# Head attention of a perceiver block: the values written straight into the projection's layout instead of through copies and moves

## The reference

```
qkv = x @ Wqkv.T + bqkv                      # x: layernorm of the rows, 8 x 64 x 512
qkv = qkv.reshape(B, 16, S, 96)              # a plain reshape: no transpose of heads
q, k, v = split(qkv, 3)                      # 32 numbers each
attn = softmax(q @ k.T / sqrt(32))
vals = (attn @ v).reshape(B, S, 512)
x = x + vals @ Wo.T + bo
```

## Time and profile before

| | us |
|---|---|
| three timed executions | 916.1, 907.73, 914.78 (median 914.78) |
| the profiled execution | 909.06 |
| its span, first to last instruction | 907.3 |
| head attention in it | 702.9 to 779.0 |
| granted TensorE clock, mean of the span | 0.932 |
| busy: PE, DVE, ACT, POOL | 770.9, 598.9, 365.4, 162.7 |

### The profile page before, as it was taken

The page is one execution under the profiler, slowest core; times in us unless marked ns, Lnnn a source line. Parts: engine busy times, 40 slices in busy tenths (PEclk is TensorE's granted clock), DMA queues, the critical chain, the costliest instruction groups (busy, mean ns, idle before and its releaser), DMA issues. The chain is left out here.

```text
span 907.3 us, 37926 instructions
## 1 busy us (share of the span) xinstructions
PE 770.9 (85%) x17278; PEld 642.7 (71%) x17278; DVE 598.9 (66%) x1152; ACT 365.4 (40%) x732; POOL 162.7 (18%) x431
## 2 busy tenths in 40 slices
PE   5697779998989999979998989796788887749995
PEld 2544779998989998979998889796644764324442
DVE  3877457776775876784876785637565878783325
ACT  3776425333525334434334431101157763352331
POOL 3020210411321311311211311101001013140003
PEclk9799889999999999999999999999889788779998
DMA  9976990365291553490463490602294701643425
GB/s 334 375 156 120 263 161 5 56 91 171 42 206 70 77 102 139 64 242 12 67 114 137 65 180 4 143 4 94 85 359 105 233 13 25 207 138 91 122 80 152
DMA packets 180187, 115.76 MB, mean 128 GB/s; under 512 B 146556, under 2 KB 158900, under 8 KB 176828
## 3 DMA queue, kind: packets, MB, share of 16 engines
q1 hardware_dynamic: 169040, 100.85, 46.0%
q10 hardware_dynamic: 8988, 6.69, 2.4%
q0 software_dynamic: 2000, 5.80, 2.2%
HBM read 61.94 MB, written 12.85 MB: 82 GB/s over the span
## 5 line engine op out<-in xcount | busy, mean ns | idle before, releaser
L1036 PE MATMUL banks<-qa,ctxT 128*128 128x64 f16 x3744 | 117.4, 194 | 13.9 <-DVE qa L740 6.5
L1036 PEld LDWEIGHTS banks<-qa,ctxT 128*128 128x128 f16 x3744 | 114.3, 99 | 15.7 <-DVE qa L740 7.5
L987 PEld LDWEIGHTS banks<-wall,whhT 128*128 128x128 f16 x3456 | 110.0, 99 | 10.4 <-issue 3.5
L987 PE MATMUL banks<-wall,whhT 128*128 128x64 f16 x3456 | 112.0, 195 | 3.7 <-issue 2.2
L987 PE MATMUL banks<-qa,wall 128*128 128x64 f16 x3456 | 105.1, 193 | 4.2 <-DVE qa L787 2.8
L987 PEld LDWEIGHTS banks<-qa,wall 128*128 128x128 f16 x3456 | 102.5, 98 | 4.6 <-DVE qa L787 3.0
L1055 PE MATMUL banks<-qa,wall 128*128 128x64 f16 (+1 forms) x1872 | 95.2, 200 | 9.3 <-issue 6.6
L1055 PEld LDWEIGHTS banks<-qa,wall 128*128 128x128 f16 (+1 forms) x1872 | 94.0, 103 | 10.6 <-issue 10.6
L1055 PE MATMUL banks<-wall 128*128 128x64 f16 (+1 forms) x936 | 94.0, 199 | 2.3 <-issue 2.3
L1055 PEld LDWEIGHTS banks<-wall 128*128 128x128 f16 (+1 forms) x936 | 88.1, 103 | 2.4 <-issue 2.4
L88 POOL TENSOR_TENSOR wall<-wall 128x64 f32<-128x64 f32 x24 | 12.3, 513 | 349.7 <-DVE wall L83 349.7
(11 more groups left out here) (279 smaller groups left out, 1492.8 us busy)
## 6 DMA issues: line engine op xcount, KB each, us to landing
wall<-in_ctx_dram SPq DMA_DIRECT2D x17, 1024.0 KB, 10.5
wall<-in_L_ffn_routed_w_dram SPq DMA_DIRECT2D x23, 512.0 KB, 8.3
unit<-in_ctx_dram SPq DMA_DIRECT2D x6, 1024.0 KB, 7.4
xg_scratch<-room SPq DMA_DIRECT2D x1, 3840.0 KB, 20.5
y_scratch<-room ACTq DMA_DIRECT2D x15, 256.0 KB, 2.0
ctxT<-in_L_xattn_gru_wih_dram SPq DMA_DIRECT2D x3, 1024.0 KB, 17.7
ctxT<-in_L_xattn_gru_whh_dram SPq DMA_DIRECT2D x1, 3072.0 KB, 26.1
ctxT<-in_L_attn_Wqkv_dram SPq DMA_DIRECT2D x12, 256.0 KB, 8.1
```

The lines of the kernel that those rows point to most:

```text
L987: mm = pe.matmul(dst[o], a, b, start=start, stop=True, skip_group_check=True)
L1036: mm = pe.matmul(score[n][:, t * K:(t + 1) * K], a, q, start=(k == 0), stop=(k == 3 * DC - 1), skip_group_check=True)
```

## The change

`values(k)` makes for each group four products in place of one: product ii takes those columns of the turned scores that belong to quarter ii of the projection's chunk (`pT_chunks`, 32 columns in runs of 4) and writes them to partitions 32 ii to 32 ii + 31, a column tile of its own. The values of a batch then lie in PSUM as 128 partitions x 256, in one bank for each parity of k. From there `vals_high(k)` on ScalarE and `vals_low(k)` on VectorE make the two f16 halves, once for each batch in place of once for each tile. `values_out`, the 16 transfers of `move_values` and their semaphores go. `project(t)` moves in TensorE's order from batch 2t + 4 to batch 2t + 3 (ahead of that batch's values), the third of them from behind the loop into batch 7; `add_y(t)` moves on VectorE from batch 2t + 5 to batch 2t + 4. In the tail the halves of the last values stand ahead of `add_y(RT - 2)` and of the remaining chunks of weights, in place of behind two of the split tiles. The halves are written in runs of 4 f16 numbers.

```diff
--- before.py
+++ after.py
@@ -1464,14 +1464,12 @@
         prob, halves, pT = (words(big.ctxT[0])[:, i * third:(i + 1) * third] for i in range(3))
         prob, pT = (a.rearrange("p (s g q) -> p s g q", s=2, g=GB) for a in (prob, pT))
         valsS = halves.bitcast(F16).rearrange("p (s c t) -> p s c t", s=2, c=DC)
-        vals = vT
-
-        valsT = slots.rearrange("p t c r -> p (t c r)").rearrange("p (c t) -> p c t", c=DC)
-
...
         var_out, seeded, root_out, pool_done = (sem(n) for n in ("var_out", "seeded", "root_out", "pool_done"))
         var, rstd, tmp, more = (e_all.root[:, j] for j in range(4))
@@ -1479,13 +1477,15 @@
         def turn_bank(t):
             return e_all.psum[:, t % 2]
 
-        moved = [sem(f"moved{t}") for t in range(RT)]
+        def values_of(k):
+
+            return value[:, k % 2, 0:4 * 64].rearrange("p (m c r) -> p m c r", c=DC, r=4)
+
+        def values_half(k, i):
+
+            return valsS[:, i, :, 64 * k:64 * k + 64].rearrange("p c (m r) -> p m c r", r=4)
 
         block = ctx.enter_context(nc.Block())
-
-        def move_values(eng, t, ii):
-            eng.dma_start(valsT[32 * ii:32 * ii + 32, :, t * P:(t + 1) * P],
-                          vals[:, ii:HC:4, t * P:(t + 1) * P]).then_inc(moved[t], 16)
 
         @block.sync
         def _(sp):
@@ -1495,11 +1495,6 @@
...
-            for t in range(RT):
-
-                sp.wait_ge(vals_out, 4 * (t + 1))
-                for ii in range(4 if t + 1 < RT else 2):
-                    move_values(sp, t, ii)
 
         @block.gpsimd
         def _(pool):
@@ -1524,19 +1519,19 @@
             def v_in(k):
                 act.wait_ge(v_turned, k + 1)
                 if k >= 2:
-                    act.wait_ge(valued, 2 * (k - 1))
+                    act.wait_ge(valued, k - 1)
                 act.copy(v[:, k % 2].rearrange("p g e -> p (g e)"), vb[:, 0:GB * HD]).then_inc(v_out, 1)
 
             def probs_turned(k):
                 for j in range(2):
                     act.wait_ge(prob_turned, 2 * k + j + 1)
                     if k >= 2:
-                        act.wait_ge(valued, 2 * (k - 1))
+                        act.wait_ge(valued, k - 1)
                     act.copy(pT[:, k % 2, 4 * j:4 * j + 4, :].rearrange("p g q -> p (g q)"), probT[:, j, :]).then_inc(pT_out, 1)
 
-            def vals_high(t):
-                act.wait_ge(moved[t], 64)
-                act.copy(valsS[:, 0, :, t * P:(t + 1) * P], valsT[:, :, t * P:(t + 1) * P]).then_inc(vals_hi, 1)
+            def vals_high(k):
+                act.wait_ge(valued, k + 1)
+                act.copy(values_half(k, 0), values_of(k)).then_inc(vals_hi, 1)
 
             def exponentials(k):
                 act.wait_ge(shifted, k + 1)
@@ -1552,22 +1547,19 @@
                 if k + 2 < B:
                     q_block(act, h, qT, k + 2)
                 v_in(k)
+                if k >= 1:
+                    vals_high(k - 1)
                 probs_turned(k)
                 if k + 1 < B:
                     exponentials(k + 1)
                 if k + 2 < B:
                     v_block(k + 2)
-                if k >= 3 and k % 2 == 1:
-                    vals_high((k - 3) // 2)
                 if 2 <= k < B - 1:
                     wall_high(act, e_all, IN_PROJECT + k - 2, IN_PROJECT + k - 1)
-            act.wait_ge(vals_out, 4 * RT)
-            for ii in range(2, 4):
-                move_values(act, RT - 1, ii)
+            vals_high(B - 1)
             wall_high(act, e_all, IN_PROJECT + B - 3, IN_PROJECT + B - 1)
             for t in range(2):
                 tile_high(act, e_all, turn_bank(t), t)
-            vals_high(RT - 1)
             wall_high(act, e_all, IN_PROJECT + B - 1, IN_HEADS)
             tile_high(act, e_all, turn_bank(2), 2)
 
@@ -1594,17 +1586,9 @@
                                             total[half].unsqueeze(2).to_broadcast([64, GB, 64]), ALU.mult)
                     ins.then_inc(prob_out, 1)
 
-            def values_out(k):
-                for j in range(2):
-                    dve.wait_ge(valued, 2 * k + j + 1)
-                    t0 = 64 * k + 32 * j
-                    dst = vals[:, :, t0:t0 + 32].rearrange("e c (m r) -> e m c r", r=4)
-                    dve.tensor_copy(dst, value[0:HD, j, :].rearrange("e (m c r) -> e m c r", c=HC, r=4)).then_inc(vals_out, 1)
-
-            def vals_low(t):
-                dve.wait_ge(vals_hi, t + 1)
-                dve.tensor_tensor(valsS[:, 1, :, t * P:(t + 1) * P], valsT[:, :, t * P:(t + 1) * P],
-                                  valsS[:, 0, :, t * P:(t + 1) * P], ALU.subtract).then_inc(vals_lo, 1)
+            def vals_low(k):
+                dve.wait_ge(vals_hi, k + 1)
+                dve.tensor_tensor(values_half(k, 1), values_of(k), values_half(k, 0), ALU.subtract).then_inc(vals_lo, 1)
 
             def add_y(t):
                 dve.wait_ge(y_done, t + 1)
@@ -1631,20 +1615,17 @@
                     dve.wait_ge(e_all.rw_hi, 1)
                     dve.scalar_tensor_tensor(e_all.rw16[:, :, 1], e_all.rw[:], WS, e_all.rw16[:, :, 0], ALU.mult, ALU.subtract)\
                         .then_inc(e_all.rw_lo, 1)
-                if k >= 5 and k % 2 == 1:
-                    add_y((k - 5) // 2)
+                if k >= 4 and k % 2 == 0:
+                    add_y((k - 4) // 2)
                 if k >= 1:
-                    values_out(k - 1)
-                if k >= 3 and k % 2 == 1:
-                    vals_low((k - 3) // 2)
+                    vals_low(k - 1)
                 if k >= 3:
                     wall_low(dve, e_all, IN_PROJECT + k - 3, IN_PROJECT + k - 2)
-            values_out(B - 1)
+            vals_low(B - 1)
             add_y(RT - 2)
             wall_low(dve, e_all, IN_PROJECT + B - 3, IN_PROJECT + B - 1)
             for t in range(2):
                 tile_low(dve, e_all, turn_bank(t), t)
-            vals_low(RT - 1)
             wall_low(dve, e_all, IN_PROJECT + B - 1, IN_HEADS)
             add_y(RT - 1)
             tile_low(dve, e_all, turn_bank(2), 2)
@@ -1670,17 +1651,18 @@
 
             def values(k):
                 pe.wait_ge(v_out, k + 1)
-                for j in range(2):
-                    pe.wait_ge(pT_out, 2 * k + j + 1)
-                    if k >= 1:
-                        pe.wait_ge(vals_out, 2 * (k - 1) + j + 1)
-                    for g in range(4):
-                        mm = pe.matmul(value[0:HD, j, g * P:(g + 1) * P], v[:, k % 2, 4 * j + g, :],
-                                       pT[:, k % 2, 4 * j + g, :], start=True, stop=True)
-                    mm.then_inc(valued, 1)
+                if k >= 2:
+                    pe.wait_ge(vals_lo, k - 1)
+                for g in range(GB):
+                    if g % 4 == 0:
+                        pe.wait_ge(pT_out, 2 * k + g // 4 + 1)
+                    for ii in range(4):
+                        mm = pe.matmul(value[32 * ii:32 * ii + 32, k % 2, 32 * g:32 * g + 32], v[:, k % 2, g, :],
+                                       pT_chunks[:, k % 2, g, ii], start=True, stop=True)
+                mm.then_inc(valued, 1)
 
             def project(t):
-                pe.wait_ge(vals_lo, t + 1)
+                pe.wait_ge(vals_lo, 2 * (t + 1))
                 if t >= 1:
                     pe.wait_ge(y_out, t)
                 n = 0
@@ -1695,10 +1677,9 @@
                 turn_probs(k)
                 if k + 2 < B:
                     head_scores(pe, h, kT, k + 2)
-                if k >= 4 and k % 2 == 0:
-                    project((k - 4) // 2)
+                if k >= 3 and k % 2 == 1:
+                    project((k - 3) // 2)
                 values(k)
-            project(RT - 2)
             pe.wait_ge(shifted, B)
             for t in range(2):
                 turn_tile(pe, c, e_all, turn_bank(t), t)
```

More of the change, by code:

```diff
@@ L1466, in head_attention @@
         valsS = halves.bitcast(F16).rearrange("p (s c t) -> p s c t", s=2, c=DC)
-        vals = vT
-        valsT = slots.rearrange("p t c r -> p (t c r)").rearrange("p (c t) -> p c t", c=DC)
-        bo_in, zeroed, v_ready, v_turned, v_out, expd, prob_out, prob_turned, pT_out, valued, vals_out, \
+        pT_chunks = pT.rearrange("p s g (h c ii r) -> p s g ii h c r", h=2, ii=4, r=4)
+        bo_in, zeroed, v_ready, v_turned, v_out, expd, prob_out, prob_turned, pT_out, valued, \
             vals_hi, vals_lo, y_done, y_out, bo_added, dve_done = (sem(n) for n in (
                 "bo_in", "zeroed", "v_ready", "v_turned", "v_out", "expd", "prob_out", "prob_turned",
-                "pT_out", "valued", "vals_out", "vals_hi", "vals_lo", "y_done",
+                "pT_out", "valued", "vals_hi", "vals_lo", "y_done",
                 "y_out", "bo_added", "dve_done"))
```

## The result

The changed kernel takes 905.69 us (median of 16 runs, 899.53 to 912.15), the kernel before, in the same comparison, 912.77 us (16 runs, 907.73 to 919.49). The ratio is 0.9928 with a 95% interval of 0.9907 to 0.9950: faster, by 0.5 to 0.9%, so the whole interval lies within the 1% that the prediction called "same". The forecast was 903, and 905.69 lies in its range, but "faster" by more than 1%, which it held the likeliest (0.51), didn't come. The profiled executions took 909.06 before and 905.73 after, with spans of 907.3 and 904.0. The saving was 7 us in place of 9.1, and the rest of this document is mostly about why it wasn't 9.1 and what came to light on the way.

A forecast was written before the change was run, and what follows sets the result against it. No engine was full; the softmax's circle, 4.85 us by itself, was lengthened by VectorE's copies, waits for high halves and TensorE's gaps. Saving 9.1 us, 6.6 at the last product and 2.5 in the tail, counted from 911.9: 903, range 894 to 912.

The forecast's parts named there:

- same: Whole kernel: outcome within about 1%, 9.1 us, which is what a measurement can tell; chance 0.40.
- within the 30 ns: 64 columns streamed in turn: Value products on TensorE: even if the four tiles work one after another, 30 ns a record covers it.
- the slower one: Rival, value products on TensorE: records 65 ns apart, 2.24 us more a batch, 8.8 us slower, about 921; chance 0.09.
- The clock stays up because the gaps are gone: TensorE through the stage: longest idle time about 1 us, so the clock stays up in the sum.
- a projection of 5 us in the loop: TensorE in the loop: sign that would make the prediction wrong; every loop projection was expected near 2.7 at clock 1.00.
- half kept: Rival: clock falls once or twice, 3.6 us each, or 8-byte runs cost 3.4; saving 3 to 8, about 906; chance 0.18.
- Exponential to last product at the end: Last batch: exponential 0.63, sum and scaling 2.36, transposes 1.2, projection 2.65, products 2.1, together 8.95 us.
- Tail: VectorE and ScalarE after the last product: halves, `add_y`, chunks and routing, with handoffs 14.6 us; 2.5 saved there.
- A plain period: Loop batch without a projection: ScalarE's work sets the period, 5.1 us, above the softmax circle's 4.85.
- The 8-byte runs: Halves written 4 f16 numbers at a time: taken as costing nothing, with 3.4 us kept for the range.
- The moved projection: TensorE, projection one batch earlier: third no longer holds up `add_y`, fourth is hidden by nine chunks; tail saves 2.5 us.
- The period with a projection: Odd loop batches: bound by TensorE, projection 2.65 and products 2.1 included, 7.1 us to the next exponential.

The follow-up runs named there:

- e7: Changed kernel plus unread 512-column products wherever TensorE waits (end of the block before, start, loop, tail), clock held; 899.70 us, ratio 0.9839.
- e8: Kernel before plus unread 512-column products at the start and in the loop, none in the tail; 909.72 us, ratio 0.9966.
- e1: Changed kernel with the 32 value products of a batch reordered, four in a row on the same column tile; 908.37 us, ratio 0.9967.
- e9: Changed kernel with projections and additions back in their old places, plus unread products at the start and in the loop; 897.66 us, ratio 0.9846.
- e12: Changed kernel plus 8 unread value products of the old 128-column form, once behind the first batch's products; 905.61 us, ratio 0.9938.
- e4: Kernel before plus unread 512-column products only at the start, with an added wait for their weights; 916.50 us, ratio 1.0053.
- e10: Changed kernel with projections and additions back in their old places, no unread products; 900.16 us, ratio 0.9905.
- e2: Changed kernel plus unread 512-column products only at the start, with an added wait for their weights; 908.45 us, ratio 0.9967.
- e3: Changed kernel plus unread 512-column products at the start and in some waits of the loop; 900.60 us, ratio 0.9892.
- e11: Changed kernel, projections and additions in their old places, unread products at the start, in the loop and in the tail; 893.00 us, ratio 0.9834.

## Why the prediction was right, and where it was not

**The mechanism was right in the main.** With the clock equal in both kernels the change is worth 10.4 us of stage, forecast 9.1 (e7, e8), and the periods and the tail came near the terms where the clock was up. That the removed copies are what shortens the softmax's circle is read from the traces; no run parts them from the shorter products. That the time of the whole fell into the range is in part luck: two terms were wrong, and their errors had opposite signs.

**The products were mis-sized, to the good.** The 64 records of a batch were summed at 30 ns, 2.1 us. They stand 9.0 or 13.0 ns apart, 0.76 or 1.08 us. The step that failed here is the last: "within the 30 ns: 64 columns streamed in turn". The prediction looked for a distance by the width of the weights alone; e1 shows that even on one tile it is 21, and that being on different tiles is worth more than the width. Worth up to 1.3 us a batch, it is why exponential 2 came 11.77 us after the start of the stage and not 13.13. The rival that fell hardest is the slower one, which needed 48 ns.

**"The clock stays up because the gaps are gone" was wrong.** It is the step that cost the forecast, and a sign that the prediction had named for itself, a projection of 5 us in the loop, came twice. From exponential 2 to 4 it took 12.14 us (summed 10.6), with transposes and scores of 1.97 where 1.1 was taken; from 4 to 5 9.63 (7.1), with a projection of 5.30; from 6 to 7 9.11 (7.1), with one of 5.05. The gaps weren't gone. TensorE waits for VectorE's scaling still (1.40 us at 740.49), where the sum had about 1 us "as between 714 and 730", and the longest that ended there was 0.59. Its own shorter products make the gap longer: with the longer ones of e1 it is 1.04, and the clock stays up. The early part has another reason: from the first transposes to the first projection there was no idle time over 0.55 us, and the clock was low all the same. The sum took over from the trace of before that the clock is up from about 714 on, without asking what had raised it there; it rose in the first batch's long products, which the change takes away. The timeline of TensorE before has them, and the idle time of 0.59:

```profile
710.13 3.25 PE L1678 MATMUL banks<-ctxT,wall 128*32 128x128 f32 x16
...
716.68 1.91 PE L1678 MATMUL banks<-ctxT,wall 128*32 128x128 f32 x16 [0.59 <-DVE wall L1602]
```

So the mix that had 1.00 for 16 us was not the same mix. The rival "half kept", with the clock as its cause, had it right and got 0.18.

**The steps one by one.** Exponential to last product at the end: 9.15, summed 8.95, but with a projection of 4.00 for 2.65, which the short products paid back. Tail: 14.73, summed 14.6. ScalarE's high half 0.38 (0.37), VectorE's low half 0.42 (0.42); its busy time fell by 10.0 us (9.6 summed). A plain period at the high clock: 4.93 (5.1). The 8-byte runs: nothing, as taken. The rule that the prediction quoted from the Trainium skill (SBUF — State Buffer, on the DMA port swizzle) asks for two or more accesses in a line; a run of four numbers makes four, and 0.38 and 0.42 agree with it. The transfers: no run keeps them, so their price isn't shown. Together: 71.46 in place of 66.9 (76.04 less 9.1), a mixture of -1.4 up to exponential 2 and +5.9 behind it.

**The moved projection** was given 2.5 us of gain in the tail and none of loss elsewhere; by the profiles of e7 and e9 the tail's gain is 2.0, and the loop pays 4.0 for it at a held clock. The period with a projection was summed at 7.1; it is 6.0 with the clock held (6.04 and 5.95 in e7), since the products are 1.3 shorter, and 9.1 to 9.6 as the clock was. What the old order would have made of the new products wasn't asked.

**Open.** What in TensorE's work the clock goes by isn't settled: 32-column products and transposes over 22 of 23 us left it low, and wide ones raised it in e12 but at first not in e4; no run varied one property alone. Whether e10 beats the changed kernel is within the intervals. Outside the stage the profiles differ by up to 10 us (828.2 in e10, 837.8 in e7); of this only the next block's start is explained.

## What to carry to other kernels

When a change replaces long TensorE operations by short ones, or closes a wait, price the stage at both clocks and look up which operation brought the clock up before: what the change is worth at a held clock (10.4 us) and what came out (4.6 to 7.3) differ by that. Cheaper products can give back most of what they save: they leave longer gaps (1.40 us here, 1.04 in e1), and the clock fell behind the longer one. Four 32-column products on the four column tiles, ordered so that neighbours lie on different tiles, can be cheaper than one product of 128 columns, and can put a result straight into the layout that the next step wants. Where TensorE stands for more than a microsecond at a time and its clock is seen to fall behind that, unread wide products in the gaps are worth a try, in all of them and not only at the start (e2, e4): here they took the ratio from 0.9928 to 0.9839, and in the old order of the projections from 0.9905 to 0.9834.

## What the runs showed of the hardware

- The records of 32-column products in f32, two for each product, start 9.0 ns apart on changing column tiles at 2.4 GHz and 13.0 at 1.2 GHz; on one tile 21 and 32.5. Low to high is a ratio of 1.4 and 1.5, not the 2 of the clocks.
- A TensorE whose records cover 22 of 23 us can stay at 1.2 GHz (after), also with two rows of 128-column products of 3.6 us in a gapless stretch (e4); one with 1.0 for the whole stage had records in 57.45 of 61.9 us (e7).
- Idle times of 1.40, 1.41, 2.27 and 2.49 us each came ahead of a fall from 2.4 to 1.2 GHz (e12, e2, e3, e4); with at most 0.76 in the stage it stayed (e7, e11), and in e8 it outlasted one of 1.27. Length alone doesn't decide: in the next block of e7 it outlasted one of 1.54:

```profile
777.30 0.24 PE L1438 MATMUL banks<-e_rw,unit 128*128 128x16 f16 x4 [1.54 <-DVE unit L1428]
...
777.50 2.75 PE L2108 MATMUL banks<-ctxT,unit 128*128 128x512 f16 x12
```
